# Sixteen words of padding ahead of the stationary operands in the expert stage of a mixture-of-experts layer

## The reference, cut to what matters

```python
shared_out = _swiglu(x, shared_w1, shared_w2)
gates = softmax(x @ wg.T);  w_topk, idx_topk = top_k(gates, 8)
buf = zeros((64, 160, 512)).at[se, rank].set(x[st], mode='drop')
h = einsum('ech,efh->ecf', buf, expert_w1)          # 3072 rows of weights
x1, x2 = split(h, 2, axis=-1)
out = einsum('ecf,ehf->ech', x1 * silu(x2), expert_w2)
return shared_out + combined                        # each row times its gate, added by token
```

## The kernel before

| buffer | role | address | mod 64 | mod 512 |
|---|---|---|---|---|
| `XSh`, `XSl` | moving halves | 106240, 122624 | 0 | 256 |
| `e_WH`, `e_WL` | moving halves | 155392, 179968 | 0 | 256 |
| `e_GTh`, `e_GTl` | stationary in `down` | 204544, 208640 | 0 | 256 |
| `e_XEh`, `e_XEl` | stationary in `project` | 212736, 216832 | 0 | 256 |
| `e_XEo`, `e_SLo`, `e_GFo`, `e_GTo`, `e_tick` | small ones | 220928 to 224000 | 0 | several |
| `b_XTh`, `b_XTl` | stationary in the first part of stage b | 88864, 72480 | 32 | 288 |
| `b_WP` | moving in stage b | 105248 | 32 | 288 |
| `b_ATh`, `b_ATl` | stationary in `project_out` of stage b | 209952, 214048 | 32 | 32 |
| `a_PR` | stationary in the transposes of stage a (L336), rows of 1032 bytes | 138080 | 32 | 352 |
| `ident` | moving in all transposes | 32896 | 0 | 128 |

## Time and profile before

### The profile page before, as it was taken

How to read it: one execution, slowest core, us unless ns; L and a number is a source line. 1 busy time by engine, 2 the same in 40 slices (tenths; PEclk the granted TensorE clock), 3 DMA queues, 4 the chain that set the end, 5 groups by cost and what they waited for, 6 DMA issues and landing times.

```text
span 2455.4 us, 50749 instructions
## 1 busy us (share of the span) xinstructions
PE 2398.7 (98%) x20730; PEld 1950.8 (79%) x20730; DVE 1941.4 (79%) x1831; ACT 1687.5 (69%) x2121; POOL 597.8 (24%) x475
## 2 busy tenths in 40 slices
PE   7989899999999999999999999999999999999998
PEld 4667787778888888888888888888888888888886
DVE  6764676667999899989788989988778878866895
ACT  6743433356887788878677878877677767766784
POOL 1210200012322342223223322223222222212221
PEclk9999999999999999999999999999999999999999
DMA  7830232357999999999889989989888878878894
GB/s 269 287 143 2 108 116 89 139 213 303 374 390 354 348 375 389 380 325 376 306 322 348 372 328 380 381 325 357 292 316 322 322 291 325 323 279 293 327 349 137
DMA packets 126018, 716.84 MB, mean 292 GB/s; under 512 B 15584, under 2 KB 23904, under 8 KB 49920
## 3 DMA queue, kind: packets, MB, share of 16 engines
q1 hardware_dynamic: 100096, 670.09, 69.8%
q0 software_dynamic: 25600, 41.96, 8.4%
HBM read 686.49 MB, written 25.49 MB: 290 GB/s over the span
## 4 chain that ended last, share of the span: by engine, by line
PE 78%; issue 0%; POOL 0%; DVE 0%; ACT 0%; ACTq 0%; POOLq 0%; DVEq 0%
PE ps L1709 14%; PE ps L1711 14%; PE ps L1710 14%; PE ps L1787 7%; PE ps L1789 7%; PE ps L1788 7%; PE ps L1740 5%; PE ps L1759 4%; PE ps L1772 3%; PE ps L1696 1%; PE ps L1750 1%; PE ps L1699 0%; POOL out_rows L1672 0%; POOL out_rows L1670 0%; DVE e_XEl L1623 0%
## 5 line engine op out<-in xcount | busy, mean ns | idle before, releaser
L1601 DVE TENSOR_TENSOR e_WL<-ring,e_WH 128x2048 fp32r<-128x2048 f32 x231 | 528.9, 2290 | 118.4 <-ACT e_WH L1521 116.4
L1601 DVE TENSOR_TENSOR XSl<-ring,XSh 128x2048 fp32r<-128x2048 f32 x229 | 524.1, 2289 | 108.6 <-ACT XSh L1521 106.7
L1521 ACT ACTIVATE e_WH<-ring 128x2048 fp32r<-128x2048 f32 x231 | 442.4, 1916 | 54.9 <-PE ps L1711 28.2
L1521 ACT ACTIVATE XSh<-ring 128x2048 fp32r<-128x2048 f32 x229 | 438.7, 1916 | 54.0 <-PE ps L1711 28.6
L1658 POOL TENSOR_TENSOR e_tick<-e_tick 128x1 f32<-128x1 f32 x126 | 112.2, 890 | 1301.0 <-ACT X L1569 1183.7
L1709 PE MATMUL ps<-e_WH,e_XEh 128*128 128x512 f32 x920 | 362.0, 393 | 0.0
L1711 PE MATMUL ps<-e_WH,e_XEl 128*128 128x512 f32 x920 | 358.7, 390 | 0.0
L1710 PE MATMUL ps<-e_WL,e_XEh 128*128 128x512 f32 x920 | 358.2, 389 | 0.0
L1601 DVE TENSOR_TENSOR e_WL<-e_more,e_WH 128x2048 fp32r<-128x2048 f32 x114 | 260.9, 2289 | 53.1 <-ACT e_WH L1521 52.0
L1709 PE MATMUL ps<-XSh,e_XEh 128*128 128x512 f32 x616 | 243.0, 394 | 4.5 <-DVE e_XEl L1623 4.5
L1711 PE MATMUL ps<-XSh,e_XEl 128*128 128x512 f32 x616 | 240.9, 391 | 0.0
(11 more groups left out here) (247 smaller groups left out, 4486.6 us busy)
## 6 DMA issues: line engine op xcount, KB each, us to landing
ring<-in_experts SPq DMA_DIRECT2D x462, 1024.0 KB, 8.2
e_more<-in_experts SPq DMA_DIRECT2D x114, 1024.0 KB, 8.1
ring<-in_shared SPq DMA_DIRECT2D x12, 1536.0 KB, 6.8
a_K<-in_ctx_k SPq DMA_DIRECT2D x32, 514.0 KB, 4.9
a_V<-in_ctx_v SPq DMA_DIRECT2D x32, 512.0 KB, 6.0
X<-in_x SPq DMA_DIRECT2D x4, 512.0 KB, 5.0
a_VL<-in_ctx_l SPq DMA_DIRECT2D x32, 64.0 KB, 5.1
xn_scratch<-ring SPq DMA_DIRECT2D x1, 2048.0 KB, 8.3
```

What stands on the lines that cost most here:

```text
L1521: act.activation(halves(nth)[0], unit(i), ACT.Copy).then_inc(hi_done, 1)
L1601: dve.tensor_tensor(l, unit(place(kind, n)), h, ALU.subtract).then_inc(lo_done, 1)
```

## The change

One buffer of 16 floats (64 bytes in each partition) is allocated behind `e_WL`. Nothing reads or writes it. All buffers behind it, `e_GTh` to `e_tick`, lie 64 bytes further on: `e_GTh` at 204608, `e_XEh` at 212800. `XSh`, `XSl`, `e_WH`, `e_WL`, `ring` and `e_more` stay where they are. No instruction, wait, size or order is changed; only the addresses in operands are.

```diff
             WH = sb("e_WH", [P, HELD - EARLY, UNIT], F32R)
             WL = sb("e_WL", [P, HELD - EARLY, UNIT], F32R)
+            apart = sb("e_apart", [P, 16])
             GTh = sb("e_GTh", [P, 2, G, P], F32R)
             GTl = sb("e_GTl", [P, 2, G, P], F32R)
             XEh = sb("e_XEh", [P, 2, G, P], F32R)
```

## The result

The changed kernel takes 2495.78 us, the median of 4 runs (2494.38 to 2496.98); before, measured beside it, takes 2461.2 us (2460.8 to 2461.97). The ratio is 1.0147, with a 95% interval of 1.0133 to 1.016: 34.6 us more, for 64 bytes that nobody reads.

The account below looks back on a forecast made before the run. TensorE's 6912 stage e matmuls times their pitch were taken to bound the kernel. No instruction changes, writers 0 us and pitch 0 us left the median at 2461.5 us; the range was 2408 to 2493 us, with 0.86.

Parts of the forecast that it names:

- What bounds the kernel: TensorE's matmuls, busy 98% of the span; time is 6912 stage e matmuls times their pitch, 226.5 ns.
- There is something in a pitch to win or lose: Stage e matmuls: 226.5 ns measured against 213.3 ns for 512 columns at 2.4 GHz; 13.2 ns lost at full clock alone.
- With nothing beside them: Stage e matmuls at clock 0.5: the 426.7 ns pitch read as 512 columns at 1.2 GHz without anything alongside.
- No cost through the writers: ScalarE and VectorE reads and writes of the moved tiles: same elements, same steps, 0 us.
- The bound of the pitch by the nearest rows: Stage e pitch at 64 bytes taken from rows at distances 0 and 256: 226.5 to 227.0 ns, so 0 us.
- the row at a distance of 256 bytes: Stage b, stationary operand from `b_ATh` at 32, moving one at 288: 227.0 ns, taken as no difference.
- The row at common remainder 288: Stage b, both operands at 288 by 512: 226.6 ns, taken to show that the common position doesn't matter.
- The transposes of stage a: L336 reads `a_PR` at many small distances to `ident`: loads 141 and 140 ns, matmuls 273 and 273, no difference.
- The argument that joined them: Load and stream run at different rates, so a 64-byte shift moves a collision's moment, hardly the number: 0 us.
- Rival 2: Slower: the shift keeps stage e matmuls out of a favourable phase, 4.5 ns each, 31 us, 2493 us; chance 0.16.
- Rival 1: Faster: load and stream reads in stage e no longer collide, up to 13.2 ns each, 2408 us; chance 0.18.
- What would show each step: Row of 24 matmuls, L1709 to L1711: 5.21 us if unchanged, 4.9 us for Rival 1, 5.31 us for Rival 2.

Follow-up runs that it names:

- experiment 5: Stationary operand of `project` cut to 64 columns: 2469.81 us against the kernel before's 2459.07; the same cut in the changed kernel, 2490.55 us.
- The sweep: Kernel before with other paddings, putting operands of `project` and `down` at distances of 32 to 384 bytes: 2462.82 to 2491.44 us, beside 2459.07 to 2460.86.
- experiment 1: Kernel before with the 64 bytes of padding ahead of `e_WH`, so `e_WH` and `e_WL` move too, `XSh` and `XSl` stay: 2478.36 us beside 2460.86.
- experiments 1 and 7: For 7: `e_XEh` and `e_XEl` moved by 16 bytes against the kernel before, 2469.82 us beside 2460.06; experiment 1 has its own line.

## Why the prediction was wrong

**What bounds the kernel: right.** TensorE's chain has all of the time, so that a change of the pitch comes out in the kernel's time. 6.6 ns for each of 6912 matmuls would be 45.6 us. The traces have 36.0, because steps behind transposes were slow before and grew less, and the medians differ by 34.6. One reading was off: behind "at full clock in every slice" stands a digit 9, which is 90% or more, and the stretch in the earlier trace rows has 0.50.

**There is something in a pitch to win or lose: right as far as it goes.** The loss at the full clock is not fixed; it is 13.3 ns at distance 0 and 20.0 ns at 64. At half the clock it is nothing at either. "With nothing beside them" isn't what those rows show: weight loads are busy for 2.00 of 2.50 us there, beside the stream, and cost it nothing. That it is a competition of two reads for SBUF is likely, since the distance between them decides, but not shown. The half load (experiment 5) speaks against its simple form.

**No cost through the writers: right**, 682 to 685 ns and 592 ns.

**The bound of the pitch by the nearest rows: this step failed.** I took the row at a distance of 256 bytes for one that speaks on 64. The sweep shows a period of 256, so that 0 and 256 are one and the same case, and my two rows were one. The row at common remainder 288 was distance 0 again. No row of float32r matmuls had another distance. The transposes of stage a had, and ran like those at distance 0; that told nothing of float32r matmuls. The argument that joined them failed as well: "A start 64 bytes on then moves the moment of a collision, and hardly the number." The rates came from rows; that the number stays the same came from none, and the term of the sum that hung on it, 0 ns for each of 6912 matmuls, measured 5.4 ns in the mean and 6.6 under way, 36.0 us in the trace. What the runs put in its place is that the distance decides, within one row of matmuls (experiment 1), and that the moment matters: at 16 bytes a row of matmuls keeps the rhythm in which it was entered.

**Rival 2 was the outcome.** Its mechanism, a favourable phase that a distance of 64 keeps the array out of, fits experiments 1 and 7, and isn't shown beyond that. Its size was taken from the pitch behind transposes, 4.5 ns and 31 us. Measured are 6.6 ns on rows under way, and less on the 255 chains behind transposes (192 of `down`, 63 of `project`), since those were slow before: ten steps of `down` took 2309 ns there and 2335 now. The range ended at this rival's own centre, 2493, and the result lay 2.8 us above. A range that counts a rival with 0.16 should not end in the middle of it.

**Against the rival I set the row of 256 bytes once more.** The same row thus weighed twice, on the forecast and against the rival, and it was empty both times.

**The other points.** Rival 1, a gain, is out: no distance tried went under 226.7 ns under way. The Trainium skill's rule ("SBUF — State Buffer", section "Who interferes with whom"), that TensorE's two read ports are independent and TensorE never waits on anyone, asks for one time at all distances; the trace disagrees, with 233.3 and 226.3 ns in experiment 1 and 34.6 us in the time. I had said that I didn't rest on it, but the forecast was the one that it gives. What would show each step was put rightly: a row of 24 in 5.31 us for rival 2, and 233.0 ns a step make 5.36.

## What to carry to other kernels

Where float32r matmuls with a load each are on the path, put streamed and stationary operands at the same address modulo 256 bytes, and look at the pitch of an unbroken row: 226.7 ns for 512 columns was the best that any placement gave here. A small buffer allocated between them can cost 1.5%, so pad small buffers to 256 bytes or allocate them last. And before a row is used as the nearest one, ask whether it differs from today's case in the thing that the change moves, or only by a period of it.

## What the runs showed of the hardware that I had not expected

- At the full clock the pitch of float32r matmuls of 512 columns with a load each depends on the distance of the two operands, with a period of 256 bytes as far as tried: 226.7 ns at 0, 229.1 at 192, 231.6 to 233.6 at the others from 32 to 224 and at 384.
- At a granted clock of 0.50 it doesn't: 426.7 ns at 0 and at 64.
- At a distance of 16 bytes there are two steady pitches, 227 and 233 ns, and the way in decides: 127 rows at the one, 63 at the other.
- A stationary operand of fewer columns isn't cheaper for the stream: 226.7 ns with 128 columns, 230.0 with 96 and with 64, though the load fell from 188 to 161 and 135 ns.
- Open: which unit makes the two wait for each other, whether it is the operand in the array or the one being loaded that counts, and what sets the value at each distance. The runs tell that a moment in time is part of it, not which.
